# A decoder layer on one core: query transposes by DMA, and a new order of every engine's steps

## The reference

```
x = layernorm(x + attention(x))          # 16 heads of 8 channels, rotary positions, softmax over 128 keys
x = layernorm(x + cross(x, ctx))         # q, k, v = projections to 8 channels
    corr = mean over batch and channels of ifft(fft(q) * conj(fft(k)))   # 128 lags
    weights = softmax(top 11 of corr); R = sum of weights * roll(v, -lag)
    result = R repeated 16 times @ Wout + bout
x = layernorm(x + experts(x))            # 8 experts 128 -> 256 -> 128, gate takes the top 2
    result = gamma * (y - mean) / sqrt(var + eps) + beta,  y = mixed + x
```

## Time and profile before

| | us |
|---|---|
| median of 3 runs | 293.64 (293.58 to 296.63) |
| the profiled execution's own time | 292.44 |
| its span in the trace | 290.6 |
| PE busy | 234.6 |
| DVE busy | 194.6 |
| POOL busy | 146.4 |
| ACT busy | 137.2 |

### The profile page before, as it was taken

The page is one execution under the profiler, slowest core; times in us unless marked ns, Lnnn a source line. Parts: engine busy times, 40 slices in busy tenths (PEclk is TensorE's granted clock), DMA queues, the critical chain, the costliest instruction groups (busy, mean ns, idle before and its releaser), DMA issues.

```text
span 290.6 us, 7351 instructions
## 1 busy us (share of the span) xinstructions
PE 234.6 (81%) x2734; PEld 191.7 (66%) x2734; DVE 194.6 (67%) x539; ACT 137.2 (47%) x222; POOL 146.4 (50%) x249
## 2 busy tenths in 40 slices
PE   1645678998997998657776799999999999999910
PEld 1434466776775776545535669988997899789910
DVE  0012567899998798885464164698868887884794
ACT  1355467777787585533212475119412940292000
POOL 3566685788879675433121103534643364333552
PEclk9999979999999899995799799999999999999985
DMA  6734433110011011000000000000100010001001
GB/s 165 214 113 123 123 94 87 21 27 12 12 17 19 0 21 15 11 11 11 0 0 3 0 0 2 0 0 1 38 3 1 0 36 0 0 0 38 0 0 37
DMA packets 15311, 9.14 MB, mean 31 GB/s; under 512 B 5776, under 2 KB 14000, under 8 KB 15280
## 3 DMA queue, kind: packets, MB, share of 16 engines
q1 hardware_dynamic: 10384, 3.77, 6.3%
q10 hardware_dynamic: 4896, 4.95, 5.9%
HBM read 6.62 MB, written 1.05 MB: 26 GB/s over the span
## 4 chain that ended last, share of the span: by engine, by line
PE 45%; issue 16%; DVE 15%; ACT 7%; POOL 5%; DMA 2%; DVEq 1%; POOLq 0%; ACTq 0%; SPq 0%
PE scoreT_pair L847 8%; PE score_pair L847 7%; PE bank L861 6%; PE scoreT_pair L861 6%; PE bank L712 3%; PE bank L681 3%; ACT early L545 3%; DVE x_ext L1144 3%; PE bank L716 3%; ACT kT_all L540 2%; DMA qT_all<-mT 2%; DVE scaled L1130 2%; POOL rs L374 2%; PE score_pair L662 1%; PE scoreT_pair L675 1%
## 5 line engine op out<-in xcount | busy, mean ns | idle before, releaser
L910 DVE TENSOR_REDUCE rowmax<-score_pair 128x8 f32<-128x1024 f32 x32 | 39.0, 1220 | 8.2 <-PE score_pair L662 8.2
L545 ACT ACTIVATE early<-scoreT_pair 128x1024 f32<-128x1024 f32 x32 | 32.8, 1026 | 17.0 <-PE scoreT_pair L675 16.9
L466 POOL TENSOR_TENSOR four<-scaled 128x512 f32<-128x512 f32 x16 | 20.4, 1277 | 35.9 <-DVE scaled L1130 35.9
L861 PE MATMUL bank<-w,early 128*128 128x128 f32 x256 | 30.1, 276 | 0.0
L861 PE MATMUL scoreT_pair<-w,early 128*128 128x128 f32 x256 | 29.9, 275 | 0.0
L861 PEld LDWEIGHTS bank<-w,early 128*128 128x128 f32 x256 | 29.5, 192 | 0.3
L861 PEld LDWEIGHTS scoreT_pair<-w,early 128*128 128x128 f32 x256 | 29.2, 192 | 0.0
L847 PE MATMUL score_pair<-x2T_part,w_part 128*128 128x512 f32 x96 | 27.7, 419 | 1.5 <-DVE x2T_part L1113 1.5
L712 PE MATMUL bank<-early,v_pad 128*32 128x128 f32 x512 | 28.8, 301 | 0.1
L716 PE MATMUL bank<-early,table 128*32 128x128 f32 x512 | 28.0, 294 | 0.0
L681 PE MATMUL bank<-ident,stack 128*128 128x128 bf16 x256 | 22.5, 239 | 6.9 <-POOL stack L365 6.9
(11 more groups left out here) (166 smaller groups left out, 486.9 us busy)
## 6 DMA issues: line engine op xcount, KB each, us to landing
w<-in_w ACTq DMA_DIRECT2D x1, 1024.0 KB, 7.9
qT_all<-mT SPq DMA_DIRECT2D x32, 32.0 KB, 2.3
out<-qkv_all SPq DMA_DIRECT2D x3, 256.0 KB, 2.3
early<-in_xT ACTq DMA_DIRECT2D x1, 512.0 KB, 4.1
early<-in_ctxT ACTq DMA_DIRECT2D x1, 512.0 KB, 5.4
table<-in_tables ACTq DMA_DIRECT2D x1, 405.0 KB, 5.9
table<-in_tables ACTq DMA_DIRECT2D x1, 256.0 KB, 3.1
early<-in_xT SPq DMA_DIRECT2D x1, 256.0 KB, 5.9
```

Of the source, the lines that this page charges most:

```text
L466: pool.tensor_tensor(four[:, :], scaled[:, n % 2, 0, :], scaled[:, n % 2, 1, :], ALU.add)\
L545: act.activation(prob[n % 2][:, 2 * u:2 * u + 2, :, :], scoreT_pair[:, :].rearrange("p (i j s) -> p i j s", i=2, j=QUAD), ACT.Exp, scale=S ...
L861: mm = pe.matmul(expert_bank[k % 4][:, e4 * D:(e4 + 1) * D], hT[:, f, n * P:(n + 1) * P], w2[:, f, :], start=(c == 0), stop=(c == CH - 1))
L910: dve.tensor_reduce(rowmax[:, H // 2 * u:H // 2 * (u + 1)], score_pair[:, :].rearrange("p (r t) -> p r t", t=S), AX_X, ALU.max).then_inc(s ...
```

## The change

The diff is long, because helpers move. What it does:

- Queries are no longer transposed by PE and copied by DVE. One DMA on SP (`q_transpose`) transposes the 128x1024 bfloat16 query part of `stack` straight into `qT`, once the third piece and the second copy are written and the old contents have been used. `scores` waits for it, and `first_piece(n)` waits for the one of batch n-2.
- The order of parts in the loops of PE, DVE, ACT and POOL is new. `weighted` comes in two halves, with `scores`, `scoresT` and the transpose of maxima between; `divide` is parted in reciprocal and division, the row statistics in three parts. Normalised rows come three steps later; `y1`, `mv1` and `rs1` are four deep. `cross_residual` leaves the loop for steps 22 to 24, its last call goes behind `pre(0)`.
- The maxima's transpose uses a slot of the output bank instead of the queries' bank.
- `rope_products`, `rope_sum`, `remainder` and `third_piece` take the engine as an argument; batch 0 runs on DVE, all others stay on POOL. Pieces of maxima and normalised rows take an engine too, and stay on DVE.
- The query, key and value weights are loaded first on ACT's queue instead of SP's; x and W1 change places; the column mean comes after the first product; PE starts with 7 unused products, and then turns the output projection before the first queries.
- W1 is cut in quarters, the high part by ACT in steps 17 to 20, the low part by POOL in steps 19 to 22.
- `stay_busy` gets 4 products ahead of the query spectrum, 4 ahead of the first transposes of the expert part and 3 behind them; 2 and 3 stand as before.

```diff
+WARM_UP = 7
...
-        y1 = [sb(f"y1{i}", [P, D + XC]) for i in range(2)]
+        y1 = [sb(f"y1{i}", [P, D + XC]) for i in range(DEEP)]
...
-            sp.dma_start(wqkv[:, 0:3 * D], a["wqkvT"]).then_inc(s["attn_w"], 16)
             load(sp, 0)
             load(sp, 1)
...
+            def q_transpose(n):
+
+                wait(sp, s["scoreT"], 2 * (n - DEEP + 1))
+                sp.wait_ge(s["mid_copy"], n + 1)
+                sp.wait_ge(s["lo"], n + 1)
+                sp.dma_start_transpose(out=qT[n % DEEP][:, :, :], in_=stack[n % 2][:, 0:H * SLOT]).then_inc(s_qT[n % DEEP], 16)
+
...
-            for k in range(B + 5):
+            for k in range(B + 6):
                 if live(k - 4):
-                    spread_maxima(k - 4)
+                    q_transpose(k - 4)
+                if live(k - 6):
+                    spread_maxima(k - 6)
...
-        maxima_slot = qkv_bank[:, QKV:QKV + S // 2].bitcast(BF16)
+        maxima_slot = out_bank[:, 2 * D:2 * D + S // 2].bitcast(BF16)
...  # POOL
+            def w1_low_piece(i):
+                pool.wait_ge(s["w1_high"], i + 1)
+                pool.tensor_tensor(w1_part[:, 1, w1_quarter(i)], w1[:, w1_quarter(i)], w1_part[:, 0, w1_quarter(i)].bitcast(F32), ALU.subtract)\
+                    .then_inc(s["w1_low"], 1)
...
+            for k in range(B + 10):
+                if live(k - 1) and k > 1:
+                    rope_products(pool, k - 1)
+                if live(k - 2) and k > 2:
+                    remainder(pool, k - 2)
+                if live(k - 6):
+                    if k == 6:
                         pool.wait_ge(s["v_cleared"], 2)
+                    pad_v(k - 6)
+                    small_columns(k - 6)
+                if live(k - 1) and k > 1:
+                    rope_sum(pool, k - 1)
+                if live(k - 2) and k > 2:
+                    third_piece(pool, k - 2)
+                if live(k - 10):
+                    inverse_deviation(k - 10)
+                if k % GT == 1 and (k - 5) // GT in range(G):
+                    residual((k - 5) // GT)
+                if k - 19 in range(4):
+                    w1_low_piece(k - 19)
+                if k - 22 in range(G):
+                    expand_v(k - 22)
+                if k == 22:
+                    cross_residual(0)
...
             pre(0)
+            cross_residual(G - 1)
             pre(1)
...  # ACT
+            act.dma_start(wqkv[:, 0:3 * D], a["wqkvT"]).then_inc(s["attn_w"], 16)
...
-                wait(act, s["q_tr"], n - 1)
+                wait(act, s["k_tr"], n - 1)
+                if n >= 2:
+                    act.wait_ge(s_qT[(n - 2) % DEEP], 16 * landed(n - 2))
...
+            for k in range(B + 6):
                 if live(k - 2):
-                    kT_copy(k - 2)
+                    second_copy(k - 2)
+                if live(k - 6):
+                    softmax_exp(k - 6, 1)
                 if live(k):
                     keep_qkv(k)
                 background_load(k)
+                if live(k - 1):
+                    first_piece(k - 1)
                 if live(k - 4):
                     mT_copy(k - 4)
                 if live(k - 5):
+                    softmax_exp(k - 5, 0)
+                if live(k - 2):
+                    kT_copy(k - 2)
                 if live(k - 1):
                     second_piece(k - 1)
+                if k - 17 in range(4):
+                    w1_high_piece(k - 17)
...  # PE
                     pe.wait_ge(s["k_T"], n + 1)
-                    pe.wait_ge(s["q_T"], n + 1)
+                    pe.wait_ge(s_qT[n % DEEP], 16 * landed(n))
...
+            def turn_projection():
 
                 pe.wait_ge(s["proj_w"], 16 * n_proj_w)
                 pe.wait_ge(s["first_ident"], 16)
+                pe.transpose(folding[:, 0:D], wo[:, 0:D], ident)
+                pe.transpose(folding[:, D:2 * D], bias[:, B_OUT, :], ident).then_inc(s["turned"], 1)
...
             pe.wait_ge(s["mean_ready"], 1)
-            pe.wait_ge(s["cross_w"], 32)
-            pe.matmul(out_bank[:, 0:XC], mean_w[:, :], xwq[:, :], start=True, stop=True).then_inc(s["col_mean"], 1)
+            stay_busy(WARM_UP, mean_w)
             pe.wait_ge(s["attn_w"], 16)
+            for k in range(B + 7):
+                if k == 0:
+                    turn_projection()
+                if live(k - 6):
+                    scoresT(k - 6, 1)
+                if live(k):
+                    qkv(k)
+                if k == 4:
+                    fold_cross_query()
+                if live(k - 7):
+                    project(k - 7)
+                if live(k - 6):
+                    weighted(k - 6, 0)
+                if live(k - 3):
+                    scores(k - 3, 0)
+                if live(k - 5):
+                    scoresT(k - 5, 0)
                 if live(k - 4):
+                    maxima_transpose(k - 4)
+                if live(k - 6):
+                    weighted(k - 6, 1)
                 if live(k - 2):
                     k_transposes(k - 2)
                 if live(k - 3):
+                    scores(k - 3, 1)
+            key_spectrum()
+            stay_busy(4, ident4)
             pe.wait_ge(s["q_nat"], 1)
...
+            stay_busy(4, ident4)
             x2_transpose(0)
+            stay_busy(3, ident4)
+
+            pe.wait_ge(s["w1_low"], 4)
...  # DVE
+            dve.wait_ge(s["rope_tables"], 16)
+            rope_products(dve, 0)
+            rope_sum(dve, 0)
+            remainder(dve, 0)
+            third_piece(dve, 0)
+            for k in range(B + 10):
+                if live(k - 6):
+                    reciprocal(k - 6)
                 if live(k - 7):
+                    mean_and_variance(k - 7)
                 if live(k - 6):
                     divide(k - 6)
+                if live(k - 10):
+                    normal_rows(dve, k - 10)
+                if live(k - 3):
+                    maxima(k - 3, 1)
+                if live(k - 6):
+                    residual_sum(k - 6)
+                if live(k - 3):
+                    pieces_of_maxima(dve, k - 3)
+                if live(k - 6):
+                    statistics_of_rows(k - 6)
+                if k == 0:
+                    keep_turned()
+                if k == 3:
+                    keep_folded()
                 if live(k - 2):
+                    maxima(k - 2, 0)
```

More of the change, by code:

```diff
@@ L228, in build_program @@
         s_x = [sem(f"x_in{i}") for i in range(len(LOADS))]
+        s_qT = [sem(f"qT_in{i}") for i in range(DEEP)]
         s_m = [sem(f"m_in{i}") for i in range(DEEP)]
@@ new lines, in rope_sum, with remainder @@
+        def rope_sum(eng, n):
+            eng.wait_ge(s["rope_prod"], 3 * n + 3)
+            wait(eng, s["hi"], n)
+            wait(eng, s["rest_ready"], n)
+            eng.tensor_tensor(qk[:, :], rot[:, 0, :], rot[:, 1, :], ALU.add).then_inc(s["qk_rot"], 1)
+        def remainder(eng, n):
+            eng.wait_ge(s["hi"], n + 1)
+            wait(eng, s["lo"], n)
+            wait(eng, s["mid_copy"], n)
+            eng.tensor_tensor(heads(rest[:, :]), heads(qk[:, :]), piece(n, 2 * HD, 0), ALU.subtract)\
+                .then_inc(s["rest_ready"], 1)
@@ new lines, in third_piece, with pieces_of_maxima @@
+        def third_piece(eng, n):
+            eng.wait_ge(s["rest_ready"], n + 1)
+            eng.wait_ge(s["mid"], n + 1)
+            eng.tensor_tensor(piece(n, HD, 4 * HD), heads(rest[:, :]), piece(n, 0, 3 * HD),
+                               ALU.subtract).then_inc(s["lo"], 1)
+        def pieces_of_maxima(eng, n):
+            eng.wait_ge(s["maxed"], 2 * (n + 1))
+            wait(eng, s["m_tr"], n)
+            rows = rowmax[:, :].rearrange("p (u a j) -> p u a j", u=2, a=2)
+            eng.tensor_copy(maxima_columns(0), rows).then_inc(s["max_rows"], 1)
+            eng.wait_ge(s["max_rows"], 2 * n + 1)
+            eng.tensor_tensor(maxima_columns(1), rows, maxima_columns(0), ALU.subtract).then_inc(s["max_rows"], 1)
@@ L534, in second_piece, with second_copy @@
                 act.activation(piece(n, 0, 3 * HD), heads(rest[:, :]), ACT.Copy).then_inc(s["mid"], 1)
-                act.activation(piece(n, 5 * HD, 5 * HD), heads(rest[:, :]), ACT.Copy).then_inc(s["mid"], 1)
+            def second_copy(n):
+                act.activation(piece(n, 5 * HD, 5 * HD), heads(rest[:, :]), ACT.Copy).then_inc(s["mid_copy"], 1)
             def kT_copy(n):
@@ L637, in _, with stay_busy @@
         def _(pe):
+            def stay_busy(n, tile):
+                for _ in range(n):
+                    pe.matmul(bank[3][:, 0:tile.shape[-1]], mean_w[:, :], tile[:, :], start=True, stop=True)
             def qkv(n):
@@ L642, in qkv @@
                 wait(pe, s["qkv_kept"], n)
-                wait(pe, s["m_T"], n - 4)
                 if n == 0:
                     pe.matmul(qkv_bank[:, 0:3 * D], xT[:, n, :], wqkv[:, 0:3 * D], start=True, stop=True)
+                    pe.wait_ge(s["cross_w"], 16)
```

(11 more changed lines are left out.)

234 lines of the change are left out of this document (72 added, 162 removed).

## The result

| | before | after |
|---|---|---|
| median, us | 295.11 (293.58 to 296.63, 4 runs) | 274.34 (273.44 to 274.97, 4 runs) |
| the profiled execution | 292.44 | 273.77 |
| its span | 290.6 | 271.7 |

The ratio is 0.929, with a 95% interval of 0.922 to 0.937; the median of before includes a fourth run on the same chip, of 296.58. The kernel after was run again later and gave 274.68 and 0.938 (0.933 to 0.943), so the gain is 6 to 7%. Some executions took one or a few per cent longer, most of them at a lower granted TensorE clock; every ratio leaves them out, so that in experiment 2 it rests on two executions of ten, and the trace shown there is one of the other eight. Of the 18.9 us of span, the second maximum of batch 0 brings 2.7, the fifteen steps behind it 16.3, the drain 0.4; from the last normalised rows to the end it is 0.5 longer.

The account below looks back on a forecast made before the run. No engine was full, so order and hand-offs set the step, TensorE and DVE close behind. From 292.4 us, start and loop took 21.7, drain 1.2, behind it +2.1: 271.6; with 1.2 for the median 273, range 262 to 288.

Parts of the forecast that it names:

- The step: Loop over batches: a quiet step falls from 6.06 to 5.2 us, the average from 6.47 to 5.5, ends 5.1 and 6.3.
- The floor: Loop: the largest busy time of an engine bounds a quiet step, at 4.9 to 5.1 us.
- The 0.3 for the residual steps: Loop: average addition per step for steps with bias additions on POOL, 0.3 us against 0.41 in the kernel before.
- Rival A: Loop: hand-offs don't shorten or SP's issue takes 3.5 us; step stays at 6.3, total 285 us; chance 0.22.
- The start: Until batch 0's second maximum: 24.5 us against 31.74, ends 22 and 28.5.
- The transpose: Query DMA on SP: lands in about 4 us, between a low end of 4 and a high end of 18.4.
- Rival B: Query DMA: runs block by block, 10 us to land, step 8.0, total 310 us, slower than before; chance 0.14.
- Room for the landing: Loop: up to 6 or 7 us of the query DMA's landing are free before the next first piece waits.
- The drain: Last batch's second maximum to last normalised rows: about 16.1 us against 17.35, 1.2 less.
- The cover on POOL: Drain: POOL's idle 4 us a step covers W1's low quarters and three bias additions; failing costs 1 to 3 us.
- Behind the drain: After the last normalised rows: busy-keeping products cost more than the faster clock returns, together +2.1 us, ends -1 and +4.
- the forecast's own signs: First maximum near 22.5 us, DVE over 90%, query landing 3 to 6, no spread wait at transposed scores, drain near 16.

Follow-up runs that it names:

- experiment 2: Kernel before with queries transposed by one DMA on SP and the old order of all steps: median 298.08 us, ratio 1.008.
- Experiments 1: Kernel after with queries again transposed by TensorE and copied by DVE, in the new order: median 286.92 us, ratio 0.980.
- Experiment 5: Kernel after with three 1 MB background loads (last eight sequences, W1, W2) issued in later steps: median 277.85 us, ratio 0.955.
- the combined versions: Kernel after, output projection turned in step 2 and POOL's last rows ahead of bias work; loads late, unchanged or W1 and W2 quartered: 271.39, 269.05, 268.51 us.
- experiment 4: Kernel after with three spare DMA transposes of the queries added per batch, into unread tiles: median 324.09 us, ratio 1.101.
- experiment 3: Kernel after with one spare DMA transpose of the queries added per batch, into an unread tile: median 284.47 us, ratio 0.975.
- experiment 6: Kernel after with two value expansions and one bias addition on POOL moved behind the last inverse deviation: median 273.70 us, ratio 0.940.
- the second run: Second run of the unchanged kernel after; its trace has a drain of 19.0 us, against 17.6 in the profiled one.
- experiment 7: Kernel after without the eleven unused products that the change adds behind the loop: median 275.86 us, ratio 0.945.
- experiment 8: Kernel after with keys also transposed by DMA on the same queue, without their TensorE transposes and ACT copy: median 283.69 us, ratio 0.970.
- the second combined version: Kernel after with output projection turned in step 2 and POOL's last rows ahead of bias work, loads unchanged: median 269.05 us, ratio 0.921.

## Why the prediction was right, and where its terms were off

The forecast was 273, the median 274.34; against the profiled execution 271.6 and 273.77. The mechanism held: with both parts, the busiest engine sets the step. That the total came within 2.2 us of the profiled execution is in part luck. The start comes out 4.6 us later than forecast and the drain 0.8 longer; the fifteen steps take 1.8 less and what is behind the drain 1.6 less.

- **The step** was put at 5.2 quiet and 5.5 on average, and is 5.16 and 5.38. The floor was TensorE's, put at 5.08 and measured 5.16; the forecast took its 5.2 from DVE instead, with a margin of 0.3, so the number was better than its ground. Experiments 1 and 2 show what stood behind it: with the query transposes gone and the old order the step is 6.02, with the order alone 6.16. The 0.3 for the residual steps was right as a size (0.22) and not as a cause: a bias addition costs its step 0.2 us at most, and most of the excess is the one step in which TensorE is still slow. The kernel before has early long steps too: its first three (6.55, 6.91 and 6.75 us) make 2.0 of its 6.1 us over fifteen quiet ones, and only one bias addition lies in them (38.04), so the forecast's reading that the additions are what exceeds 6.06 was wrong for this third of it. Rival A (6.3) fell, as TensorE has no idle time left in a quiet step.
- **The start** was the failed size: 7.2 us forecast, 2.7 found. The copy of the first product came at 13.74 as put (13.6), the last piece ended at 18.55 (17.4), and the landing took 7.71 in place of 4. The forecast had named up to 4 more beside the load of x and yet took none. It named the wrong load, too: x was issued at 13.29 and took 6.4 us, so it landed about a microsecond into the transpose; what runs beside the first transpose are the last eight sequences (issued at 18.29 and 18.71) and W1 (21.50). Experiment 5 shows that it is these loads: with them moved away, 3.17. What was missed too is that turning the projection in step 0 puts its loads ahead of the first queries for no gain; the combined versions get 4.5 us from moving it.
- **The transpose** was put at 4 us from the spreads and a price per packet; the median is 3.3. Its issue was put near 0.8 and is 1.25, and TensorE is full all the same. The Trainium skill (Advanced Engine Details and Errata, section X-Bar Transpose (TRN2)) gives transposing DMAs the rate of regular ones, 350 to 400 GB/s, by which it would land in an estimated 3 us. The trace agrees, with 3.0 at the least, but most of this is the fixed part taken from the spreads (2.3 us to landing), so it is no test of the rate.
- **Rival B** fell. Eight blocks one after the other would have taken 10 us to land and 8 a step. The Trainium skill's 1309 ns for a 128x128 bf16 block by DMA (VectorE: DVE Perf Modes, section The three transpose paths) can't be multiplied by eight: a whole 128x1024 transpose lands in 3.3. A step of 8.0 came only with four transposes a batch (experiment 4).
- **Room for the landing**, put at 6 to 7 us, was right for a quiet step (one spare: 5.15) and too generous on average: what fails first is not the first piece's wait but the spread behind it on the same queue (experiment 3).
- **The drain** was put 1.2 shorter and is 0.4. The cover on POOL failed for one instruction: the bias addition at 124.63 holds the last inverse deviation, and experiment 6 gets 1.2 us back by order alone. The forecast's price for a failing cover was 1 to 3. In the trace of the second run, with its lower clock there, the drain is no shorter than before at all.
- **Behind the drain** +2.1 was forecast, +0.5 found, 0.3 of it up to the cross queries. The +1.6 of products ahead of the query spectrum is not there: the four unused products (eight instructions) end at 126.63, before the late rows are ready, so they cost nothing. From the cross queries to the first hidden product it is 1.7 us longer than before, where 2.55 were put for the products there, and the rest is 1.5 shorter, where 2.0 were put for the clock. One product was read as 0.87 us from a row that says 1.88 for two; the eight instructions now take 3.60, 0.90 each. Against no added products at all, experiment 7 gives them 4.0 us in the traces and 1.2 to 1.5 in the medians.

In the forecast's own signs: the first maximum at 22.5 is 27.13; DVE over 90% is 93%; the landing between 3 and 6 is 3.3, but for the first; between 45 and 105 us a spread's landing is named in one wait of 0.2 us; the drain near 16 is 17.

## What to carry to other kernels

Here, taking load off an engine that was not full changed nothing until the order let the engines overlap. So read the ring first, then the busy times, and expect that the two parts of such a change can be worth more together than apart. A transfer that an engine waits for should be priced beside the loads that run at the same time, and a margin that one has named for it belongs in the sum when those loads are certain to be there. On an engine with slack, the order of its last items still decides: put what the critical path waits for ahead of what nobody needs yet.

## What the runs showed of the hardware

**One DMA transpose** of 128x1024 bf16 takes 1.24 to 1.48 us to issue on SP and lands in 3.0 us at the least and 3.3 in the median, counted from the start of its issue. Beside loads of 512 KB and 1 MB the first one took 6.2 to 8.2 us in the traces read, and in experiment 8 a key transpose behind the one of the queries 10.4.

**Some DVE operations last as long as a POOL operation beside them, others don't.** Timeline of the kernel after: a cast alone and beside a bias addition, a row normalisation (0.34 alone, in experiment 1 at 72.51) beside a part of W1, and row statistics beside a bias addition:

```profile
30.33 0.19 DVE L367 CAST mstack<-rowmax 128x16 bf16<-128x16 f32 x1
35.48 1.28 DVE L367 CAST mstack<-rowmax 128x16 bf16<-128x16 f32 x1
...
114.08 1.41 DVE L373 TENSOR_SCALAR x_all<-y,mv,rs 128x136 f32<-128x136 f32 x1
119.53 0.29 DVE L981 BATCH_NORM_STATS2 st<-y 128x6 f32<-128x128 f32 x1
```

```profile
35.45 1.27 POOL L421 TENSOR_TENSOR x_ext<-x_ext,bias 128x512 f32<-128x512 f32 x1
114.12 1.28 POOL L433 TENSOR_TENSOR w_part<-w,w_part 128x512 fp32r<-128x512 f32 x1
119.50 1.26 POOL L426 TENSOR_TENSOR x_all<-x_all,bias 128x512 f32<-128x512 f32 x1
```

The cast takes 1.28 in place of 0.19 and the normalisation 1.41 in place of 0.34; the statistics take the 0.29 that they take alone, and the maxima 1.23 with an addition of 1.27 beside them (80.35). Work that is put on an idle POOL is thus not always free for a DVE on the chain; part of the missing gain in the drain may be this. It was not tried by itself.

**TensorE is slow for the first 43 us or so.** Eight score products take 0.61 us from 26.48 to 38.84, 0.54 at 43.50 and 0.40 from 45.92 on, and two products of 392 columns take 1.67 at 39.80 and 0.93 at 46.48, although the granted clock in the records is 1.00 all the time. In the second combined version the scores take 0.61 at 21.95 and 23.88, and the record says 0.50 from 10 to 35 us, the lower of the two levels (1.2 GHz). The lengths agree, the two records don't. The seven unused products at the start did not keep the later ones from it in either trace.
